# Scan tiles of 4 states by 32 channels, states added by 32-column strip products, dt spread through DRAM

## The reference, cut to what matters

```python
u, z = split(seq @ in_proj_w.T)              # 256 channels each
u = silu(conv4(u) + conv_b)
dt, Bm, Cm = split(u @ x_proj_w.T)           # 8, 16, 16
dt = softplus(dt @ dt_proj_w.T + dt_proj_b)  # 256 channels
h = exp(dt * A) * h + (dt * u) * B           # 256 channels x 16 states, place after place
y = sum over the states of h * C, + u * D    # then y * silu(z) @ out_proj_w.T
```

## Time and profile before

| | us |
|---|---|
| median of 2 runs (2604.11 to 2607.12) | 2605.61 |
| span of the profiled execution | 2602.9 |
| its own time beside the span | not recorded apart; the median of the runs is 2.7 above the span |
| VectorE busy | 1314.5 (51%) |
| TensorE busy | 2384.9 (92%) |
| GpSimd busy | 1232.4 (47%) |
| ScalarE busy | 1018.9 (39%) |

### The profile page before, as it was taken

How to read it: one execution, slowest core, us unless ns; L and a number is a source line. 1 busy time by engine, 2 the same in 40 slices (tenths; PEclk the granted TensorE clock), 3 DMA queues, 4 the chain that set the end, 5 groups by cost and what they waited for, 6 DMA issues and landing times.

```text
span 2602.9 us, 28352 instructions
## 1 busy us (share of the span) xinstructions
PE 2384.9 (92%) x7648; PEld 1242.0 (48%) x7649; DVE 1314.5 (51%) x2016; ACT 1018.9 (39%) x2041; POOL 1232.4 (47%) x1086
## 2 busy tenths in 40 slices
PE   4788989888898898888999999999999999999995
PEld 3445545555455554544444444444444444444443
DVE  1899999999999999992321111111111111111112
ACT  3777877778777787762110111101111101111110
POOL 2889999999999999983051000011111111111110
PEclk8999999999999999999999999999999999999997
DMA  4122222222222222221003000331313132231116
GB/s 173 52 72 64 80 71 74 77 65 81 71 74 77 65 80 71 77 73 56 29 25 122 21 28 23 113 121 24 121 24 115 31 121 90 55 121 24 24 20 154
DMA packets 69266, 186.07 MB, mean 71 GB/s; under 512 B 10080, under 2 KB 15304, under 8 KB 66336
## 3 DMA queue, kind: packets, MB, share of 16 engines
q1 hardware_dynamic: 57424, 160.06, 18.8%
q0 software_dynamic: 11728, 24.73, 5.1%
HBM read 158.14 MB, written 26.62 MB: 71 GB/s over the span
## 4 chain that ended last, share of the span: by engine, by line
PE 53%; ACT 15%; issue 12%; POOL 8%; DVE 6%; DMA 4%; SPq 0%; POOLq 0%; ACTq 0%; DVEq 0%
PE pair L1497 29%; PE single L1509 16%; ACT WALL L819 6%; DVE WALL L1062 3%; DMA u<-xrows,gix 2%; POOL WALL L566 2%; PE pair L1373 2%; POOL dtu L470 1%; POOL dt L463 1%; POOL dt L466 1%; DVE pair L1050 1%; PE pair L1479 1%; ACT L665 1%; ACT L673 1%; PE pair L1520 1%
## 5 line engine op out<-in xcount | busy, mean ns | idle before, releaser
L1497 PE MATMUL pair<-WALL,z 128*128 (+1 forms) x1952 | 849.9, 593 | 3.0 <-ACT z L881 3.0
L566 POOL TENSOR_TENSOR WALL<-WALL 128x768 f32<-128x768 f32 x384 | 694.1, 1821 | 66.0 <-PE pair L1373 43.7
L1062 DVE TENSOR_TENSOR_SCAN WALL<-WALL,carry,pair 128x384 f32<-128x384 f32 x640 | 610.3, 993 | 0.1
L1497 PEld LDWEIGHTS pair<-WALL,z 128*128 128x128 f32 x1952 | 366.8, 190 | 442.5 <-issue 440.9
L1373 PE MATMUL pair<-WALL,ident 128*128 128x384 f32 x1536 | 560.0, 489 | 1.6 <-DVE pair L1050 1.0
L819 ACT ACTIVATE WALL<-dt,An 128x384 f32<-128x384 f32 x768 | 421.5, 605 | 140.9 <-POOL dt L466 136.4
L887 ACT ACTIVATE dt<-pair 128x512 f32<-128x512 f32 x122 | 72.9, 597 | 813.9 <-PE pair L1497 813.9
L1373 PEld LDWEIGHTS pair<-WALL,ident 128*128 128x128 f32 x1536 | 284.2, 192 | 149.7 <-issue 23.1
L1189 DVE SCALAR_TENSOR_TENSOR dtu<-dt,tab,pair 128x512 f32<-128x512 f32 x86 | 64.3, 747 | 549.0 <-ACT dt L887 549.0
L1198 DVE COPY absx<-pair 128x512 f32<-128x512 f32 x61 | 42.2, 692 | 393.6 <-PE pair L1520 393.6
L1509 PE MATMUL single<-WALL,absx 128*128 (+1 forms) x488 | 221.7, 597 | 2.9 <-issue 1.8
(11 more groups left out here) (228 smaller groups left out, 2257.3 us busy)
## 6 DMA issues: line engine op xcount, KB each, us to landing
WALL<-crows SPq DMA_DIRECT2D x192, 384.0 KB, 3.5
WALL<-in_L_ffn_w_dram SPq DMA_DIRECT2D x24, 2048.0 KB, 13.8
X<-in_x_dram SPq DMA_DIRECT2D x4, 1152.0 KB, 6.6
xrows<-rows SPq DMA_DIRECT2D x24, 192.0 KB, 3.5
u<-xrows SPq DMA_DIRECT2D x18, 256.0 KB, 2.7
WALL<-yrows SPq DMA_DIRECT2D x4, 1152.0 KB, 15.6
out_dram<-X SPq DMA_DIRECT2D x8, 576.0 KB, 10.5
WALL<-in_L_ffn_sw_dram SPq DMA_DIRECT2D x2, 2048.0 KB, 17.0
```

The lines of the kernel that those rows point to most:

```text
L566: pool.tensor_tensor(hC[m], hs[:, (NS * j + n) % HRING, :, :], Cs[G % 3][:, n % CG, :].unsqueeze(1).to_broadcast([P, HALF, T]), ALU.mult). ...
L1062: scan = nv.tensor_tensor_scan(hs[:, m, h, :], dA[(NS * j + n) % AHEAD][:, h, :], dBu[h], init, ALU.mult, ALU.add)
L1497: last = mm(bank[2 * w + q][:, :], xT[k][:, r, :], WALL[:, ds(off + (w * RR * I + r * I + q * 512), 512)], start=(r == 0), stop=(r == RR - 1))
```

## The change

A scan tile now holds 4 states of 32 channels (partition = 32a + channel, a the state within the group) instead of one state of 128. A loop step n still has two such tiles (e=0,1), so there are 16 steps a chunk with operations of the same sizes; step n covers 4 states of 64 channels, and 8 steps cover the 16 states of one half h. The B selector gives 4 states at once and one spread serves two steps. dt and dtu are written to DRAM (`dtd`) and read back by 4 DMAs for each half, each to 32 partitions. C rows come by 4 DMAs a chunk. The 4 states of a tile are added by a product with `fold` (128x32) into 32 partitions of Yt, 4 strips for a pair of steps, and the D*u product starts each half. Yt is one bank, and y is gated in two halves. The scan's tiles take the whole of WALL; the shared expert's weights are loaded after the last scan. Places of the front pieces: u products at n=9 to 12 and `projections` at n=14 of the chunk before (were n=14, 15 and 0, 1, and n=3); `residue` at VectorE's n=1 (was 5); `dt_product` at n=3 (was 7); SiLU of u at ScalarE's n=2 (was 6), `bc_hi` 4 (8), `bc_mid` 6 (10), `abs_relu` 8 (12), `exps` 9 (13); softplus at GpSimd's n=6 to 9 (were 9 to 12). The back of a chunk runs partly later: its centring is at n=4 of the chunk two after it (was n=14 of the chunk after), with two buffers `cen2`. In the setup TensorE moves A and the token's dt*u into the new layout by 16 products of 32 columns each.

```diff
-        dA ... WALL[:, SCAN0 + at[0]:...]        # SCAN0 = 2*I*RR: w1, w3 of the shared expert lie below
+        v = WALL[:, at[0]:at[0] + n]
+    NQ = 4; DS = P // NQ; NJ = HALF * P // DS; NPH = NS // 2
+    dtd = nc.dram_tensor("dtd", (2, 2, HALF * P, T), fp32, kind="Internal").ap()
+        dtR, dtuR = part(NJ * T), part(NJ * T)   # each as p j t
+        lnx, dt, dtu = absx, onex, expx          # one buffer each, were two of their own
-        Yt, Dt = pair[0], pair[2]
+        Yt, Dt = bank[0], pair[2]
+        M0, M1, M2 = bank[6], bank[7], bank[1]

 SyncE, per chunk (was: eight loads of 2 rows of C to all partitions, store_rows, store_c)
+                        store_c(g + 1, ...); load_c(g + 1, 1 - k)
                         store_rows(g - 3, 1 - k)
+                        store_dt(g + 1, 1 - k)          # waits f_dt
+                        store_dtu(g + 1, 1 - k)         # waits f_dtu
+                        spread_dt(g + 1, 1 - k, 0)      # waits m_dts; 4 DMAs
+                        spread_dtu(g + 1, 1 - k, 0)     # waits m_dtus; 4 DMAs
+                        spread_dt(g + 1, 1 - k, 1)
+                        spread_dtu(g + 1, 1 - k, 1)
+            def spread_rows(tile, k, which, h, done):
+                for a in range(NQ):
+                    sp.dma_start(tile[a * DS:(a + 1) * DS, h * NQ:(h + 1) * NQ, :],
+                                 dtd[k, which, h * P:(h + 1) * P, :].rearrange("(c b) t -> b c t", b=DS))
+            sp.wait_ge(m_h, NS * NCH); sp.wait_ge(m_y, NPH * NCH)     # then w1, w3, w2 of the shared expert,
+            ...                                                        # ahead of load_tile(0), load_tile(1)

 ScalarE
-                            sc.wait_ge(f_dt, g + 1)                    # n == 0
+                            sc.wait_ge(m_dtR[h], 16 * NQ * (g + 1))    # n == 0 and n == 8
-                            nsc.activation(dA[..][:, h, :], dt[k][:, h, :], ACT.Exp, scale=An[:, h, n:n + 1])
+                            nsc.activation(dA[..][:, e, :], dtR[:, h * NQ + c + e, :], ACT.Exp, scale=AnR[:, c + e, h, q:q + 1])
 VectorE
-                nv.tensor_tensor(yd[:, :, :], Yt[:, :, 0:T], z[r][:, :, :], ALU.mult)       # n == 3
+                nv.tensor_tensor(yd[:, h, :], Yt[:, 0:T], z[r][:, h, :], ALU.mult)          # h=1 at n == 3, h=0 at n == 11
-                            v.wait_ge(f_dtu, g + 1)                    # n == 0
+                            v.wait_ge(m_dtuR[h], 16 * NQ * (g + 1))    # n == 0 and n == 8
 TensorE
-                for h in range(HALF):
-                    last = mm(Yt[:, h, 0:T], ident[:, :], hC[n % RING][:, h, :], ...)        # add_y, each n
+                if q == 0: mm(Yt[:, 0:T], Dg[:, h, :], u[k][:, h, :], start=True, stop=False)
+                for c in range(NQ):                                                         # add_pair, each odd n
+                    last = mm(Yt[c * DS:(c + 1) * DS, 0:T], fold[:, :], hC[(n - 1 + c // 2) % RING][:, c % 2, :],
+                              start=False, stop=(q == NQ - 1), tile_position=(0, c * DS))
```

More of the change, by code:

```diff
@@ L336, in store_rows @@
                 sp.dma_start(xrows[ds(g * CP, CP), :], rows[:, :]).then_inc(b_out[k], 16)
-            store_c(0, 0)
+            store_c(0, 0, 0)
+            load_c(0, 0)
+            store_dt(0, 0)
+            store_dtu(0, 0)
+            for h in range(HALF):
+                spread_dt(0, 0, h)
+                spread_dtu(0, 0, h)
             def batch(b, first, last):
@@ L341, in batch @@
                     g, k = b * JC + j, j % 2
[L342 to L355, removed]
+                    if not (last and j == JC - 1):
+                        store_c(g + 1, 1 - k, b * (JC // 2) + (j + 1) // 2)
+                        load_c(g + 1, 1 - k)
+                    if not (first and j < 3):
+                        store_rows(g - 3, 1 - k)
+                    if not (last and j == JC - 1):
+                        store_dt(g + 1, 1 - k)
[4 more added lines that the diff above has]
+                        spread_dtu(g + 1, 1 - k, 1)
             batches(sp, batch)
@@ L556, in batch @@
                     behind = not (first and j == 0)
+                    late = not (first and j < 2)
                     bb, bj = (b if j else b - 1), (j - 1) % JC
+                    lb, lj = (b if j >= 2 else b - 1), (j - 2) % JC
                     for n in range(NS):
@@ L1249, in _ @@
                 te.transpose(bank[4][0:RANK, h * P:(h + 1) * P], dp_raw[:, h, :], ident[:, :])
+            for a in range(NQ):
+                for c in range(NQ):
+                    mm(bank[5][a * DS:(a + 1) * DS, c * HALF * NQ:(c + 1) * HALF * NQ], ident[:, c * DS:(c + 1) * DS],
+                       An[:, :, a::NQ], start=True, stop=True, tile_position=(0, a * DS))
             for r in range(RR):
@@ L1353, in _ @@
                     for two in range(2):
+                        u_first(0, 0, two)
+                    for two in range(2):
                         u_second(0, 0, two)
-                    for two in range(2):
-                        u_first(0, 0, two)
             projections(0, 0)
@@ new lines, in batch @@
+                        if late and n == 7:
+                            pe.wait_ge(b_sq, g - 1)
+                            mean_of(sq2, b_var, stat)
+                        if front0 and n == 13:
+                            pe.wait_ge(f_sq, g + 4)
+                            mean_of(sq, f_var, stat)
+                        if n % 2 == 1:
+                            if ph < NPH - 2:
+                                spread(g, j, ph + 2)
+                            elif front:
+                                if ph == NPH - 2:
+                                    pe.wait_ge(f_lo, g + 2)
+                                spread(g + 1, j + 1, ph + 2 - NPH)
+                            if n >= 3:
+                                add_pair(g, k, n - 2)
+                            elif behind:
+                                add_pair(g - 1, 1 - k, NS - 1)
@@ L1423, in batch @@
+                        if n == 0:
+                            if late3:
+                                pe.wait_ge(b_rows, g - 2)
+                                gate_logits(g - 3, 1 - k, M2)
+                            if late:
+                                pe.wait_ge(b_x, g - 1)
+                                mean_of(xchunk(lb, lj), b_mean, M2[:, STAT:STAT + CP])
+                        if front and n == 1:
+                            z_second(g + 1, 1 - k)
                         if front and n == 3:
-                            projections(g + 1, 1 - k)
```

451 lines of the change are left out of this document (238 added, 213 removed).

## The result

The changed kernel takes 2784.67 us (median of 2 runs, 2782.09 to 2787.25) against 2605.61: a ratio of 1.069 (95% interval 1.065 to 1.072), so it is **slower**, and by more than the range of the forecast (2612 to 2724). The profiled execution has a span of 2780.6 us, 177.7 more than before.

| part | forecast | measured |
|---|---|---|
| first residue (89.95 before) | 97.9, +8.0 | 95.48, +5.5 |
| 22 rounds from residue to residue | 48.2 each, +40.3 | 53.05 each, +147.0 |
| last residue to the end of the scans (74.8 before) | 86.7, +11.9 | 89.5, +14.7 |
| end of the scans to the first expert product (14.8 before) | 24.6, +9.8 | 24.6, +9.8 |
| the experts | 0 | +0.5 |

A forecast was written before the change was run, and what follows sets the result against it. It took a ring through all engines, lengthened by a DRAM trip from 46.37 to 48.2 us a chunk, as the bound. First chunk +8.0, 22 rounds +40.3, last residue to scan end +11.9, tail +9.8: 2676 us, range 2612 to 2724.

The forecast's parts named there:

- What bounds the kernel now: Before the change: a ring through TensorE, ScalarE, GpSimd and VectorE, 46.37 us a chunk, within 1 us of VectorE's 45.5.
- The parts off the ring: Scans, products and decays keep their counts and shapes; TensorE's 32 identity products become 32 strip products, priced serially without switch.
- VectorE's 2.7 us per slot hides it: TensorE's strips for a pair of states, 2.6 us if serial, claimed to fit within VectorE's time per slot.
- The ring after: After the change: residue, softplus, dtu, trip through DRAM, ScalarE's queue, next residue; 48.2 us a chunk against 46.37.
- all four terms: Residue to first softplus step 18.3 us, to dtu's end 12.5, to first decay 5.3, to the residue's copy 12.1.
- softplus steps alternate with three C products: 12.5: GpSimd: four softplus steps with three C products of 1.8 us between, 12.5 us until dtu is done.
- The trip of 5.3: dtu's end to spread dt landed: five issues at 0.35 us, 1.75, then 3.5 to land; bounds 2.7 and 7.0.
- two ways to the first softplus step: From the residue: GpSimd's C product of n=6 ends at 18.3 us, ScalarE's softplus inputs at 17.9; 18.3 taken.
- Setup, first chunk and tail: Outside the rounds: first residue +8.0 us with setup's +6 within, last residue to last scan +11.9, tail +9.8.
- (1): DRAM trip hidden at 2.7 us, ring 45.6, VectorE's 45.5 sets the pace: 2615 us; chance 0.25.
- (3): GpSimd or ScalarE runs ahead, so half the loss: period 46.5 to 47.5 us, some 2640 to 2660; chance 0.12.
- (2): TensorE becomes the bound: clock falls to 0.5, 2742 us, or costly serial strips, up to 2716; chance 0.18.

The follow-up runs named there:

- experiment 7: Kernel before the change with its residue at n=6 instead of n=5: 2603.87 us, ratio 0.9989 to the kernel before.
- Experiment 4: Changed kernel with the mean product over sq2 at TensorE's n=7 moved behind that slot's spread and strips: 2734.46 us.
- experiment 3: Changed kernel with VectorE's residue moved from n=1 to n=3, ahead of the gate: 2669.51 us.
- experiment 1: Changed kernel with SyncE's first spread of dt issued ahead of the store of dtu: 2738.12 us.
- experiment 11: Changed kernel with each spread of dtu issued only after its chunk's first decay: 2779.36 us.
- experiment 5: Changed kernel with dt spread before dtu's store, residue at n=3 and the sq2 mean behind the strips: 2623.88 us, 1.0065 of the kernel before.
- experiment 9: Changed kernel with dt and dtu laid out in DRAM so spreads read 6 KB pieces, each store becoming four DMAs: 2813.81 us.

## Why the prediction was wrong in size

**What bounds the kernel now**: wrong on one point. The views were read rightly and both numbers, 45.5 and 46.37, were there; but a ring that closes within 1 us of VectorE's time was called the bound, where experiment 7 shows it had slack. A chain followed back through the timelines meets the residue's input just ahead of it whether or not it is late; the missing sign was a wait on the residue's own row, and the earlier trace rows has none. It cost the sum nothing, for the 46.37 was measured, whatever set it.

**The parts off the ring**: the decision to price strips serially was on the safe side: eight of 384 columns took 0.85 us (1.51 where the clock was at its lower level), against 2.6 assumed. But "VectorE's 2.7 us per slot hides it" is the sentence that failed. It priced the strips and not the slot they stand in, and in slot n=7 they stood behind a mean product that waits for a square which the change had moved six ScalarE slots back. Experiment 4 puts it at 2.1 us a round. The same holds for slot n=13 and the front's mean product, which the change put ahead of the spread of B that VectorE needs first in a chunk (it stood at n=0); experiment 3 shows it set the pace once the residue was out of the way.

The Trainium skill, TensorEngine Tiling (Array Packing), Key Properties, says that tiles run in parallel, and 0.85 us for eight strips agrees. The drain at a change of mode that it also names isn't seen as a gap: the mean product of 643.13 (to 644.27), one spread of 0.52 at 644.07 and the strips of 644.52 follow each other without one. The profile's ends of products are modelled, so a short drain isn't excluded.

**The ring after**: the path was right in every member, and so was the queue behind dtu (experiment 1). The failed step is its sum, 48.2: **all four terms were too small**, by 0.66, 1.95, 1.23 and 0.82 us. The largest, "softplus steps alternate with three C products: 12.5", is 12.45 once the mean product is out of the way. The trip of 5.3 was priced by five issues at 0.35 us and a landing of 3.5, from loads made at a DMA share of 0.24. Here the issue of the fourth spread ends 2.4 us after dtu (1.75 said; one issue takes 0.43), and it lands 4.1 later, 4.5 from the start of its issue (3.5 said). The other twelve spreads are not the cause (experiment 11). The two other terms run through TensorE slots, at a granted clock of 0.74 where the forecast kept 1.00. Of the forecast's two ways to the first softplus step, ScalarE's, said to end at 17.9, ends at 18.7 and is now the later one. Lifting the clock to 0.91 gave back 0.5 and 0.8 us of these two. The Trainium skill, DMA: Bandwidth & Descriptors, Anatomy of one DMA, gives a price for one DMA on GpSimd's path. Used for these, which SyncE issues, and for all their bytes at once, it gives the forecast's estimate of 4.7 us for the trip. 6.53 was measured, so the case speaks against using that line for four DMAs into 32 partitions each.

**Setup, first chunk and tail**: near in sum, in part by luck. The first dtu is there at 77.06, 2.0 us later than before where the setup was priced at +6; the trip then took 6.9 us for 5.3, so the first residue was only 2.4 us earlier than said. The end of the last chunk was 2.8 later (the same slow terms), the tail within 0.1 us.

**The rivals**: (1), the hidden trip, didn't happen. (3) neither. (2) happened in part and together with the forecast, not in its place: TensorE isn't the bound (135 of 200 us busy), but its clock did fall. The reason given there, gaps left by strips side by side, is part of it: in experiment 5, with the pace as before, TensorE is busy 143.8 us for 178.4 and the clock is 0.82. The rest, to 0.74, comes with the late ring. **The range** failed for this: the cases were taken as exclusive, and the terms of one ring as if their errors offset each other. They don't. Work that is late in one member left the others idle, TensorE with more idle time ran at 0.74 (filled up, at 0.91), and both made the ring longer, so here the errors have one sign. 22 rounds times 4.85 is 107 of the 108.7 us missed. The forecast also took 2% for the least that can be told from none; the executions of one kernel here lie within some 6 us of each other.

The views the forecast named as signs did their work: residues apart, VectorE idle at the residue, ScalarE released by a DMA of dt were right in kind (52 to 54 for 48; 3.7 to 4.4 for 2 to 3; 11.5 for 9), the landing (4.5 us for the fourth spread, where 3.5 was said) and TensorE's clock and busy share were wrong. The first product of a chunk does start without a wait, but the copy ahead of it has one.

What stays open: which property of the spreads holds the full DMA share at 235 GB/s (not their piece size in DRAM, experiment 9; that each reaches only 32 partitions was not tested), and what the clock alone is worth, without the repeated products that lifted it.

## What to carry to other kernels

When a change lengthens a loop of work that passes through several engines, list every instruction queued ahead of each member in its slot, with what it waits for; one moved square cost 50 us, and three reordered queue entries gave back 161 of 179. Don't treat the terms' errors as independent, and take a transfer's price from a row made under the load it will meet. And before calling a ring the bound, look for a wait on the row of its last member. Without one it has slack there, though it may close at another instruction (experiment 3).

## What the runs showed of the hardware

- Eight strip products of 128x32 weights and 384 columns took 0.85 us with the clock at its upper level and 1.51 at the lower; eight identity products one after the other, at the pitch of 0.32 us from the earlier trace rows, take 2.6. Four strips on different columns of the array run side by side: in the group of 651.54 they start within 0.02 us of each other and each takes 0.51, and the next four follow after 0.35.
- Products repeated to raise the granted clock gave 49 us in one kernel (2784.67 to 2735.81, from 0.74 to 0.91) and cost 15 in another, whose pace VectorE set (2623.88 at 0.82, 2638.43 at 0.91).
- Sixteen spreads from DRAM to 32 partitions each held the DMA share at 1.0 with only 226 to 235 GB/s, in pieces of 1.5 KB and of 6 KB alike. Holding twelve of them back made the trip only 0.2 us shorter (6.34 for 6.53).
- A store of 384 KB to DRAM landed in 2.6 us, where the forecast took 3.5 from the stores of rows, of 192 KB.
